# Scores of four heads on four row strips in the two width-16 attentions, with a two-pair schedule

## The reference, cut to what matters

```
logits = (q @ k.T) / 4               # per batch and head: 112 x 375, contraction over 16
logits = logits + (1 - mask) * -1e9  # a2 only
attn   = softmax(logits)
attn   = attn * group_prob           # a2 only: a 112 x 375 factor of the batch
out    = attn @ v                    # 112 x 16
x      = x + tanh(gate) * (out of all heads @ Wo + bo)
```

## Time and profile before

| | us |
|---|---|
| median of three runs (lowest to highest) | 1442.02 (1438.07 to 1448.39) |
| profiled execution, time | 1443.31 |
| profiled execution, span | 1441.6 |
| first scores of a2 to last transposes of a2 | 612.67 to 788.39 |
| first scores of a3 to last transposes of a3 | 1171.49 to 1340.20 |
| TensorE busy over the span | 1206.0 (84%) |
| VectorE, ScalarE, GpSimd busy | 859.9, 686.2, 538.8 |
| mean granted TensorE clock | 0.919 of 2.4 GHz |

### The profile page before, as it was taken

One profiled execution on the slowest core, in us unless ns is written; L12 is line 12 of the kernel. 1 busy time (PEld: TensorE's weight loads), 2 busy tenths in 40 slices (PEclk: granted clock), 3 DMA queues, 4 the chain that ended last, 5 costly groups with the idle time before them and its releaser, 6 DMA issues. The chain is left out here.

```text
span 1441.6 us, 25435 instructions
## 1 busy us (share of the span) xinstructions
PE 1206.0 (84%) x9539; PEld 948.0 (66%) x9539; DVE 859.9 (60%) x1950; ACT 686.2 (48%) x1533; POOL 538.8 (37%) x538
## 2 busy tenths in 40 slices
PE   2999999999996797589999379999998079999665
PEld 2677777777774365457776378988888057777333
DVE  6664565555443246667776646666674367777474
ACT  3345543454442222256666145445552047766465
POOL 3355554555553000288887431011100440450232
PEclk9999999999997998889999579999999579999886
DMA  6000000000001151300110445556650250000000
GB/s 174 6 7 12 12 1 12 12 1 1 1 1 22 30 153 33 88 21 22 42 32 2 172 150 172 198 187 194 187 177 17 80 164 23 23 2 2 1 10 17
DMA packets 59929, 88.63 MB, mean 61 GB/s; under 512 B 8640, under 2 KB 49808, under 8 KB 59808
## 3 DMA queue, kind: packets, MB, share of 16 engines
q1 hardware_dynamic: 57696, 81.49, 18.6%
q0 software_dynamic: 2112, 5.51, 1.3%
HBM read 81.48 MB, written 5.51 MB: 60 GB/s over the span
## 5 line engine op out<-in xcount | busy, mean ns | idle before, releaser
L906 POOL TENSOR_SCALAR a_arena<-a_arena 112x487 f32<-112x487 f32 x128 | 193.0, 1519 | 176.5 <-DVE a_arena L1117 176.5
L1198 ACT ACTIVATE a_arena<-banks,a_arena 112x487 f32<-112x487 f32 x128 | 84.3, 663 | 192.3 <-DVE a_arena L1111 192.3
L1111 DVE TENSOR_REDUCE a_arena<-banks 112x2 f32<-112x974 f32 x64 | 75.0, 1172 | 102.7 <-PE banks L997 102.7
L93 PE MATMUL banks<-f_x_high,f_up_high 128*128 128x256 f32 x448 | 128.3, 286 | 3.6 <-DVE f_up_low L1981 2.2
L94 PE MATMUL banks<-f_x_low,f_up_high 128*128 128x256 f32 x448 | 127.9, 286 | 0.0
L95 PE MATMUL banks<-f_x_high,f_up_low 128*128 128x256 f32 x448 | 127.8, 285 | 0.0
L397 POOL TENSOR_TENSOR a_arena<-a_arena 112x375 f32<-112x375 f32 x128 | 114.9, 925 | 24.1 <-ACT a_arena L704 23.9
L513 PE MATMUL banks<-ident,a_arena 112*126 112x112 f32 x768 | 105.8, 275 | 12.0 <-POOL a_arena L397 9.5
L513 PEld LDWEIGHTS banks<-ident,a_arena 112*126 112x126 f32 x768 | 77.6, 144 | 46.4 <-issue 26.8
L2018 POOL DMA_INDIRECT f_arena<-f_rows,f_arena x28 | 32.1, 1146 | 194.5 <-PE banks L2051 175.0
L2162 DVE TENSOR_TENSOR f_arena<-banks,f_arena 128x512 f32<-128x512 f32 x56 | 38.4, 686 | 100.4 <-ACT f_arena L2141 100.4
(11 more groups left out here) (333 smaller groups left out, 3326.6 us busy)
## 6 DMA issues: line engine op xcount, KB each, us to landing
f_arena<-in_L_ffn_w1T SPq DMA_DIRECT2D x14, 1024.0 KB, 6.1
f_arena<-in_L_ffn_w3T SPq DMA_DIRECT2D x14, 1024.0 KB, 5.0
f_arena<-in_L_ffn_w2T SPq DMA_DIRECT2D x14, 1024.0 KB, 5.7
a_arena<-in_ctxT SPq DMA_DIRECT2D x24, 375.0 KB, 5.1
a_arena<-in_ctx SPq DMA_DIRECT2D x16, 375.0 KB
f_y<-f_arena SPq DMA_DIRECT2D x14, 256.0 KB, 5.0
a_arena<-in_L_xattn_Wkv SPq DMA_DIRECT2D x2, 1024.0 KB, 9.9
a_arena<-in_fside_BxSxS SPq DMA_DIRECT2D x8, 164.1 KB, 2.4
```

The costliest lines, as they stand in the source:

```text
L93: pe.matmul(out, sh, mh, start=start, stop=False)
L906: pool.tensor_scalar(z, z, inv[:, n % 4, s:s + 1], None, ALU.mult).then_inc(p_ready, 1)
L1111: dve.tensor_reduce(negmax[:, n % 4, :], banks[0:T, 0:2, 0:KEYS], AX, ALU.max, negate=True).then_inc(max_ready, 1)
L1198: act.activation(prob[n % PR][s][:, 0:KEYS], banks[0:T, s, 0:KEYS], ACT.Exp, bias=negmax[:, n % 4, s:s + 1], accum_out=total[:, n % 4, s:s ...
```

## The change

Both attentions now use the fused maximum with `scored`; a3 adds a block of zeros, filled once by POOL. `scores(q)` computes two pairs (four heads) at once on strips 0 to 3 and banks 0 to 3, and waits for all maxima of the two pairs before. Four engines' hand-written orders go by two pairs: PE's is `turn(n - 1)`, `scores` of pairs n + 2 and n + 3, the piece of n, `turn(n)`, `weigh`, the piece of n + 1, for even n. DVE and ACT have the maximum or exponential of one pair before and of the other after `copy_turned(n)`. POOL's `expand` moves ahead of `regroup`.

```diff
@@ -295,8 +295,10 @@
...
             neg = [m.sb(f"neg{u}", [T, KEYS]) for u in range(2)]
-            scored = [m.sb(f"scored{j}", [T, KEYS]) for j in range(4)]
-            spacers = m.sb("spacers", [T, 4])
+        else:
+            neg = [m.sb("neg", [T, KEYS])] * 2
+        scored = [m.sb(f"scored{j}", [T, KEYS]) for j in range(4)]
+        spacers = m.sb("spacers", [T, 4])
         psT, psO, psP = [banks[:, 4 + j, :] for j in range(2)], banks[:, 6, :], banks[:, 7, :]
@@ -408,6 +410,8 @@
...
                 negate_mask(0)
+            else:
+                pool.memset(neg[0], 0.0).then_inc(neg_made, 1)
             low_context(1)
@@ -416,10 +420,10 @@
...
                 b, k = n // STEPS, n % STEPS
+                if n >= 4 and n % 4 == 0:
+                    expand(n // 4 - 1)
                 if grouped and n < PAIRS:
                     regroup(n)
-                if n >= 4 and n % 4 == 0:
-                    expand(n // 4 - 1)
                 if k == 1 and grouped and b + 1 < B:
@@ -481,18 +485,17 @@
...
-            def scores(n):
-                b, i, s = n // STEPS, n // 2 % 4, n % 2
-                u, g, e = b % 2, i // 2, i % 2
-                if n % STEPS == 0:
+            def scores(q):
+                b, g, e = q // 4, q // 2 % 2, q % 2
+                u = b % 2
+                if q % 4 == 0:
                     pe.wait_ge(piece_moved, moved(("K", 1, b))[0])
-                if n % STEPS == 0:
                     pe.wait_ge(q_low, b + 1)
-                if n > 1:
-                    pe.wait_ge(max_ready if grouped else exp_done, 2 * (n - 1))
+                if q:
+                    pe.wait_ge(max_ready, 4 * q)
                 for k, (a, z) in enumerate(((0, 0), (0, 1), (1, 0))):
-                    for h, j in heads_of(n):
+                    for j in range(4):
                         r = slice(32 * j, 32 * j + 32)
@@ -553,17 +556,21 @@
...
             scores(0)
-            scores(1)
-            for n in range(LAST):
+            for n in range(0, LAST, 2):
+                if 0 < n <= PAIRS:
+                    turn(n - 1)
                 if n + 2 < PAIRS:
-                    scores(n + 2)
-                if n < PAIRS:
-                    turn(n)
-                if n >= 3 and n % 2 and n < PAIRS + 2:
-                    weigh((n - 3) // 2)
+                    scores(n // 2 + 1)
                 if n in later:
...
                     piece(later[n], 7)
+                if n < PAIRS:
+                    turn(n)
+                if 2 <= n < PAIRS + 2:
+                    weigh(n // 2 - 1)
+                if n + 1 in later:
+                    bank_free(n + 1)
+                    piece(later[n + 1], 7)
@@ -606,22 +613,17 @@
...
             def maximum(n):
-                dve.wait_ge(s_ready, n + 1)
-                j, r = 2 * (n % 2), n % 4
-                if grouped:
-                    b = n // STEPS
-                    if n % STEPS == 0:
-                        dve.wait_ge(neg_made, b + 1)
-                    if n > 1:
-                        dve.wait_ge(exp_done, 2 * (n - 1))
-                    for s in range(2):
-                        dve.memset(spacers[:, j + s:j + s + 1], 0.0)
-                        dve.tensor_tensor_reduce(scored[j + s], banks[0:T, j + s, 0:KEYS], neg[b % 2], -1.0, LARGEST,
-                                                 ALU.add, ALU.min, negmax[:, r, s:s + 1]).then_inc(max_ready, 1)
-                else:
-                    dve.tensor_reduce(negmax[:, r, :], banks[0:T, j:j + 2, 0:KEYS], AX, ALU.max,
-                                      negate=True).then_inc(max_ready, 2)
+                dve.wait_ge(s_ready, n // 2 + 1)
+                b, j, r = n // STEPS, 2 * (n % 2), n % 4
+                if n % STEPS == 0 and (grouped or b == 0):
+                    dve.wait_ge(neg_made, b + 1)
+                if n > 1:
+                    dve.wait_ge(exp_done, 2 * (n - 1))
+                for s in range(2):
+                    dve.memset(spacers[:, j + s:j + s + 1], 0.0)
+                    dve.tensor_tensor_reduce(scored[j + s], banks[0:T, j + s, 0:KEYS], neg[b % 2], -1.0, LARGEST,
+                                             ALU.add, ALU.min, negmax[:, r, s:s + 1]).then_inc(max_ready, 1)
@@ -661,21 +663,30 @@
...
             evacuate(first[5], first_bank[5])
+            def taken(n):
+                if n in later and later[n][0] != "I":
+                    evacuate(later[n], 7)
+                    if later[n][0] == "O":
+                        dve.wait_ge(piece_moved, moved(later[n])[0])
+                        follow.row(dve, later[n][2])
             maximum(0)
-            for n in range(LAST + 1):
-                if n + 1 < PAIRS:
-                    maximum(n + 1)
+            maximum(1)
+            for n in range(0, LAST + 1, 2):
                 if 0 < n <= PAIRS:
                     copy_turned(n - 1)
-                if n >= 4 and n % 4 == 0 and n <= PAIRS:
-                    invert(n // 4 - 1)
+                taken(n - 1)
+                if n % 4 == 2 and n < PAIRS:
+                    invert(n // 4)
+                if n + 2 < PAIRS:
+                    maximum(n + 2)
                 if n >= 6 and n % 4 == 2 and n <= PAIRS + 2:
                     move_out(n // 4 - 1)
-                if n - 1 in later and later[n - 1][0] != "I":
-                    evacuate(later[n - 1], 7)
-                    if later[n - 1][0] == "O":
-                        dve.wait_ge(piece_moved, moved(later[n - 1])[0])
-                        follow.row(dve, later[n - 1][2])
+                taken(n)
+                if n < PAIRS:
+                    copy_turned(n)
+                if n + 3 < PAIRS:
+                    maximum(n + 3)
@@ -697,12 +708,11 @@
...
                 for s, (h, j) in enumerate(heads_of(n)):
-                    act.wait_ge(max_ready, 2 * n + s + 1 if grouped else 2 * n + 2)
+                    act.wait_ge(max_ready, 2 * n + s + 1)
                     if n > 3:
                         act.wait_ge(t_ready, 2 * (n - 4) + s + 1)
-                    src = scored[j][:, 0:KEYS] if grouped else banks[0:T, j, 0:KEYS]
-                    act.activation(prob[n % 4 * 2 + s][:, 0:KEYS], src, ACT.Exp, bias=negmax[:, n % 4, s:s + 1],
-                                   scale=-1.0 if grouped else 1.0, accum_out=total[:, b % 2, h:h + 1]
+                    act.activation(prob[n % 4 * 2 + s][:, 0:KEYS], scored[j], ACT.Exp, bias=negmax[:, n % 4, s:s + 1],
+                                   scale=-1.0, accum_out=total[:, b % 2, h:h + 1]
                                    ).then_inc(exp_done, 1)
@@ -723,7 +733,7 @@
...
                 if b > 1:
-                    act.wait_ge(s_ready, STEPS * (b - 1))
+                    act.wait_ge(s_ready, STEPS // 2 * (b - 1))
                 act.copy(q_parts[b % 2][0][:], qm[:, :, :, b * T:(b + 1) * T]).then_inc(q_high, 1)
@@ -745,19 +755,25 @@
...
             high_context(1)
-            for n in range(LAST + 1):
-                if n < PAIRS:
-                    exponent(n)
-                if spare is not None and n in (6, 9, 12, 14):
-                    spare.scalar(act, (6, 9, 12, 14).index(n))
+            exponent(0)
+            exponent(1)
+            for n in range(0, LAST + 1, 2):
                 if 0 < n <= PAIRS:
...
                     spread(n // 4 - 1)
+                if n + 2 < PAIRS:
+                    exponent(n + 2)
+                if n in later and later[n][0] == "Q":
+                    odd(later[n], 7)
+                if n < PAIRS:
+                    copy_turned(n)
+                if n + 3 < PAIRS:
+                    exponent(n + 3)
+                if spare is not None and n in (6, 8, 12, 14):
+                    spare.scalar(act, (6, 8, 12, 14).index(n))
                 if n % STEPS == 4 and n // STEPS + 2 < B:
                     high_context(n // STEPS + 2)
-                if n - 1 in later and later[n - 1][0] == "Q":
-                    odd(later[n - 1], 7)
                 if n % STEPS == 2 and n // STEPS + 1 < B:
```

## The result

| | before | after |
|---|---|---|
| median of the runs compared (us) | 1445.2 | 1471.74 |
| lowest to highest (us) | 1438.07 to 1457.86 | 1467.54 to 1472.36 |
| ratio of the times, 95% interval | | 1.0179 (1.0132 to 1.0225) |
| span of the profiled execution (us) | 1441.6 | 1470.6 |
| a2, first scores to last transposes (us) | 612.67 to 788.39: 175.7 | 613.10 to 805.77: 192.7 |

The kernel before ran four times for this comparison; the 1442.02 of the table ahead of the prediction is the median of three of these runs. The forecast was 1425 us, with a range of 1405 to 1441. The time lies outside it, on the other side. Of the 29.0 us of longer span, 17.0 lie in a2 and 5.5 in a3. The 6.5 that are left lie where both programs do the same work: 0.4 ahead of a2, 3.6 between the attentions, 2.6 behind a3.

The account below looks back on a forecast made before the run. PE's queue bounds both loops. Per batch, -1.32 (two PE-bound iterations) + 0.12 + 0.17 (two waiting ones) = -1.03 us, 20.68 to 19.65; over 16 batches -16.5, from 1442.0 to 1425.5, stated as 1425, range 1405 to 1441.

Parts of the forecast that it names:

- The strips: PE's scores in both attentions: four heads take 0.72 us instead of 1.38, removing 0.66 us per two pairs, 42 us over 64 groups.
- Rival 3: Four strips hinder one another on PE: queue time 0.90 us, 1436.5 us; fully one after another (1.38), 1467; chance 0.06.
- The step that failed: ACT's iteration: `high_queries` and `high_context` fit behind the second exponential, since ACT is busy only 14.5 us a batch.
- Rival 4: POOL late in a2 alone, losing its 8 us (1433 us), or the clock falling in PE's new waits; chance 0.12.
- The walk of k4 and k6: Two-pair iterations at batch positions 4/5 (O, I) and 6/7 (two V): 5.17 us, +0.17; PE-bound 5.2 us, 0.66 won.
- The walk of k0 and k2: Two-pair iterations at batch positions 0/1 (I) and 2/3 (two K): 4.07 us, +0.12; PE-bound 5.2 us, 0.66 won.
- the chain through ACT: Scores, maximum, two exponentials, copy, `turn`: next scores start at 3.96 us; with DVE's delay, 4.07 at batch positions 0/1.
- Rival 2: Shared four-bank cycle x longer per iteration than walked: 1442 us at x = 0.48, 1459 at 0.75; chance 0.17.
- The fused maximum in a3: On DVE 0.95 us instead of 0.85, 6.4 us in all, inside the chain; exponentials from SBUF 0.60, as in a2.
- The clock: A clock falling in PE's new waits would cost more than 1433 us; layer 5, PE busy 44.71 of 50, keeps 1.00.

Follow-up runs that it names:

- e3: Changed kernel with ACT's query and context splits ahead of its two exponentials and bank 7 emptied before the transposes are copied: 1422.13 us, ratio 0.9855 to the kernel before.
- e7: As e3, but ACT copies the transposes of pair n between the two exponentials of pair n + 2: 1412.63 us, ratio 0.9794 to the kernel before.
- e4: Changed kernel with only POOL's order altered, low parts of queries and context two pairs later: 1455.32 us, ratio 1.0076 to the kernel before.
- e1: Changed kernel with ACT splitting context and queries ahead of its two exponentials instead of behind them: 1439.77 us, ratio 0.9959 to the kernel before.
- e2: Changed kernel with DVE and ACT emptying bank 7 before copying the transposes of pair n - 1, splits still late: 1455.14 us, ratio 1.0067 to the kernel before.
- e6: As e3, but a group's twelve matmuls queued pair by pair instead of set by set over four strips: 1422.1 us, ratio 0.9852 to the kernel before.

## Why the prediction was wrong

1. **The strips.** Right in kind and nearly in size. A group's slot was taken as 0.72 us. In the timeline after, the group that begins at 720.35 (shown above) has its other two sets and then the transposes behind it at 721.16, 0.81 on:

```profile
720.61 0.34 PE L500 MATMUL banks<-a_kT_low,a_q_high 32*112 32x376 f32 x4
720.78 0.34 PE L500 MATMUL banks<-a_kT_high,a_q_low 32*112 32x376 f32 x4
...
721.16 0.80 PE L516 MATMUL banks<-ident,a_arena 112*126 112x112 f32 x6
```

 But there the transposes' own weight load waited 0.37 us for POOL (L399). In the timelines of e3 and e7 above, transposes begin 0.78 and 0.77 us after the group (695.30 to 696.08, 697.88 to 698.65), and K 0.71 after it (699.18 to 699.89). So 0.60 to 0.67 us a group are saved, against 0.66 forecast. Rival 3 fell; its 0.90 had also scaled the slot of two strips (0.69) as if it were that of one.
2. **The step that failed: "`high_queries` and `high_context` stand at the end of ACT's iteration, behind the second exponential, where ACT (14.5 us a batch) has room."** Room on ACT was the wrong question. The moved instructions release POOL instructions that stand in POOL's queue ahead of the next `regroup`; with two pairs to an iteration, and the exponentials two pairs ahead of it, "the end" came behind the exponentials of three more pairs, while POOL's place stayed. I had the sum right (17.8 us of POOL work into a batch) and took it for the order. It cost 2.4 us a batch in a2 (after against e4), and in both attentions the late context split also held up `spread`, 0.7 us more (e1). Rival 4 named POOL, and its sign is what the trace shows (transposes that wait for `regroup` past the first batch), but it had no mechanism and priced it at a2's gain alone; the real price was more than twice that gain.
3. **The walk of k4 and k6 left out bank 7.** It followed DVE's and ACT's queues past the evacuations, but not PE's own wait ahead of a piece (`bank_free`). For k4 I had DVE done with the second K at t = 1.75 and PE at O at t = 0.72, and did not set the one against the other. O waited 1.06 us, V 1.15. In a3 k4 became 5.53 against 5.17, k6 6.31 against 5.2, and the batch 21.05 against 19.65: 1.4 us lost against the forecast. e1 and e2 give back 2.1 together.
4. **The walk of k0 and k2 held**: k0 of 3.91 to 3.92 in both attentions after, 4.07 forecast; k2 5.3, 5.2 forecast; and e7 showed the chain through ACT by shortening it. Rival 2, the slower side, named this chain, and it was not the chain: the time came out beyond rival 2's 1459 by other waits. With those gone (e3) the batch is 18.9, 0.7 below the forecast's 19.65. Most of that is k4, 4.58 against 5.17 in the walk: it is 5.5 in e1, and 4.58 in e3, where DVE empties K ahead of the copy. There DVE begins on K at 703.87, before the group at 704.34; in the walk it began 0.58 us behind the group.
5. **The fused maximum in a3**, the zeros and the exponential from SBUF cost nothing visible: DVE's busy time in a3's batch rose from 15.85 to 16.75, in an engine with 4 us of room.
6. **The clock** was rival 4's other half, put aside because layer 5 kept 1.00 with a smaller share of PE work. After, four of the twelve batches from second to seventh fell below 1.00, and one such batch cost 1.57 us (the windows at 1302.17 and 1323.24 above). e1, with the V wait at 0.5, has one such batch, and e3 none. What it adds to the 29 us was not separated by an experiment.

## What to carry to other kernels

When two loop steps are merged into one, every instruction that was "at the end of a step" lands later against the queues that were not merged (here behind three more pairs' exponentials). For each such instruction ask not whether its engine has room but what stands behind its consumer in the consumer's queue. A buffer that several small producers share (here one PSUM bank) needs its evacuations first in the new order, before copies that have slack. Busy sums give only the floor (18 us here); the time has to be walked from each engine's wait list, written down in the new order.

## What the runs showed of the hardware that I had not expected

Matmuls on disjoint row strips overlap whatever their order in the queue: twelve in the order pair by pair (e6) begin in the same three sets of four as twelve in the order set by set, and the times are the same (1422.1 and 1422.13). The kernel before shows it too: pairs 0 and 1 stand one behind the other in its queue and begin as one group. A group of four strips held the queue 0.71 us ahead of K and 0.77 to 0.78 us ahead of transposes (e3, e7), where two strips held it 0.69 us. TensorE's clock in these loops was not steady at a given amount of work: e4 did the same batch at 1.00 in 21.10 us and, right behind it, at 0.92 in 22.66 us.
